# Row maxima by DMA instead of TensorE, and two fp32 products in three rounded passes

## The chip, the cores and the metric

One NeuronCore of a Trainium2 chip runs the whole program; the other cores are idle. The metric is the device time of one execution in microseconds (us), the median over runs. The engines are TensorE (PE in the profile, its weight loads PEld), VectorE (DVE), ScalarE (ACT), GpSimd (POOL) and SyncE (SP), which here only issues DMAs.

## What is computed

The activations are `x`, 4 sequences of 256 tokens with 128 features, and a context of the same shape. Four blocks are added to `x` in turn, each after a layer norm of `x`:

```
x = x + attention0(norm(x), ctx)      # 16 heads of 8 features, softmax over 256 keys
x = x + ffn0(norm(x))                 # 128 -> 512 -> 128; butterflies of 9 stages between, exact gelu
x = x + attention1(norm(x), ctx)      # the same shape as attention0
x = x + moe(norm(x))                  # sigmoid router, best 4 of 16 experts of width 64, and a shared expert
```

The butterfly stages of ffn0 are linear, so the kernel folds them on the chip into one up weight `w_up` and one down weight `w_dn`.

## The kernel before

Everything is kept with features on the partitions and tokens along the free dimension; 1024 tokens are worked in two chunks of 512. Attention is cut into 32 **units** (`unit(U)`): layer, sequence, and a group of four heads that sit in the four 32-row quarters of the PE array. For each unit the program does, in this order:

- `maxima` ("max.U.0", "max.U.1"): four products each, queries on the output partitions, give scores in PSUM whose largest value per query is wanted;
- `reduce` on DVE ("red.U.i"): the negated maximum of each query and head, 128 x 4 values out of 128 x 1024;
- `turn`: eight fp32 products of `T` with the identity, for one or two units at once, turn these maxima from a column per head into rows, so that partition `32j+g` holds the maximum of head j; 17 turns serve the 32 units;
- `shift` on DVE: adds the turned rows to `Q` in place, where `K` has a row of ones, so the next product subtracts the maximum by itself;
- `scores` ("sc.U.0", "sc.U.1"): keys on the output partitions, with the maximum already subtracted;
- `exps` on ACT: four exponentials of 128 x 512 per unit, into `P`, which has room for three units;
- `weighted` ("pv.U"): 8 fp32 products with `V` into the bank `OB`; a copy, a shuffle, a logarithm and an exponential normalise it after each four units.

`Q` and `K` are f32r (rounded fp32), which PE takes in one pass; a plain fp32 product is two passes in the profile. Some products are split to keep precision at f32r speed: the operand is rounded (`k_hi`, `w_hi`), the remainder kept (`k_lo`, `w_lo`), and hi·hi, hi·lo and lo·hi are added in PSUM. `in_parts` does that for the experts' gate and up products. ffn0's up products (`up`), the shared expert's gate-and-up (`gate` with e = 8) and all down products of the experts (`down_product`) are plain fp32 before the change.

In the expert stage there are, for each of two chunks, eight pairs of experts: gate and up products on PE, `silu` on ACT, `prod` on DVE, `hid` (multiplication with the routing weights) on DVE or POOL, and `dn`, which adds into `OB`. `prod_t`, `hid_t` and `gate_t` have two buffers each. The routing weights reach all partitions by a store to DRAM (`comb_out`) and 16 broadcasting loads (`spread`), issued from SP.

The order on each engine is written out by hand in four lists, `PE_ORDER`, `DVE_ORDER`, `ACT_ORDER` and `POOL_ORDER`. A step waits only for the semaphores of what it needs and of the bank that it fills, but an engine never goes past a step that waits. "fill.n" stands for n products of a zero tile that nobody reads, where PE would stand idle. SP issues the first loads, and then nothing until the routing weights.

Of the kernel before, what the change touches and what calls it, by code (L numbers as in the profile page):

```python
# [45 lines left out]
PE_ORDER = """
fill.7:0 centre.0:0 kproj.0.0:1 centre.1:2 avg.0:3 kproj.0.1:4 avg.1:5 fill.1:6 qproj.0.0:6 ksel.0.0.2:0
ksel.0.1.3:3 fill.2:1 qsel.0.0.1:1 ksel.0.0.0:4 ksel.0.1.2:6 qsel.0.0.0:5 ksel.0.1.0:2 ksel.0.0.3:3
ksel.0.0.1:0 ksel.0.1.1:4 max.0.0:56 fill.1:3 max.0.1:23 max.1.0:01 kproj.1.0:4 qsel.0.0.3:5 qsel.0.0.2:6
kproj.0.2:0 max.1.1:56 max.2.0:12 centre.2:3 turn.0:4 qproj.0.1:5 avg.2:6 max.2.1:12 fill.3:3 max.3.0:56  # L50
ksel.1.0.2:3 sc.0.0:01 sc.0.1:24 turn.1:3 max.3.1:56 qsel.0.1.0:2 fill.3:1 max.4.0:34 ksel.1.0.3:1 qsel.0.1.1:2
ksel.0.2.0:0 sc.1.0:56 ksel.1.0.1:1 sc.1.1:34 fill.3:0 max.4.1:23 max.5.0:01 turn.2:6 fw.2:4 vproj.0:23
qsel.0.1.2:5 qsel.0.1.3:6 sc.2.0:01 qproj.0.2:4 fw.1:1 max.5.1:23 ksel.0.2.1:0 ksel.1.0.0:6 sc.2.1:15 pv.0
turn.3:6 sc.3.0:23 qsel.0.2.2:0 max.6.0:45 pv.1 qsel.0.2.0:1 sc.3.1:26 max.6.1:45 sc.4.0:03 pv.2 max.7.0:23
ksel.0.2.2:4 qsel.0.2.1:5 max.7.1:01 fw.0:6 sc.4.1:25 max.8.0:34 pv.3 turn.4:0 sc.5.0:12 max.8.1:56 pv.4
sc.5.1:34 max.9.0:01 ksel.0.2.3:2 kproj.1.1:5 max.9.1:34 sc.6.0:06 qsel.0.2.3:1 pv.5 sc.6.1:02 max.10.0:34
sc.7.0:16 turn.5:5 sc.7.1:02 max.10.1:34 pv.6 ksel.1.1.2:1 max.11.0:56 sc.8.0:02 max.11.1:34 pv.7 max.12.0:56
vproj.1:01 turn.6:3 sc.8.1:45 fw.3:6 sc.9.0:24 max.12.1:01 out.0.0:5 sc.9.1:34 max.13.0:01 pv.8 max.13.1:56
sc.10.0:24 centre.3:3 sc.10.1:01 sc.11.0:24 sc.11.1:56 pv.9 turn.7:0 avg.3:2 max.14.0:45 max.14.1:01 sc.12.0:36
pv.10 pv.11 max.15.0:45 max.15.1:23 up.0.0:6 up.0.3:0 up.0.2:1 up.0.1:2 sc.12.1:36 sc.13.0:45 turn.8:0 down.0:1  # L60
sc.13.1:02 sc.14.0:45 ksel.1.1.1:3 ksel.1.1.0:6 centre.5:1 sc.14.1:04 pv.12 avg.5:6 sc.15.0:25 sc.15.1:04 pv.13
pv.14 qproj.1.0:1 pv.15 ksel.1.1.3:6 qsel.1.0.0:0 fill.4:2 max.16.0:45 max.16.1:12 qsel.1.0.1:0 qsel.1.0.2:6
out.0.1:3 qsel.1.0.3:6 max.17.0:01 max.17.1:45 centre.4:2 max.18.0:01 avg.4:3 turn.9:4 fill.3:5 sc.16.0:56
max.18.1:01 max.19.0:23 up.1.3:4 max.19.1:56 up.1.2:2 up.1.1:3 up.1.0:5 max.20.0:01 sc.16.1:46 max.20.1:23
down.1:5 max.21.0:01 sc.17.0:26 sc.17.1:34 centre.6:5 turn.10:6 max.21.1:01 avg.6:2 max.22.0:45 sc.18.0:36
pv.16 turn.11:0 max.22.1:12 sc.18.1:45 qproj.1.1:3 max.23.0:56 sc.19.0:04 sc.19.1:12 pv.17 qsel.1.1.0:2
max.23.1:34 qsel.1.1.1:0 max.24.0:56 sc.20.0:12 max.24.1:34 pv.18 max.25.0:01 sc.20.1:56 turn.12:2 max.25.1:34
qsel.1.1.2:6 qsel.1.1.3:5 sc.21.0:01 pv.19 sc.21.1:36 max.26.0:01 sc.22.0:24 pv.20 max.26.1:34 sc.22.1:05
sc.23.0:16 pv.21 turn.13:2 max.27.0:34 sc.23.1:05 pv.22 max.27.1:12 sc.24.0:06 pv.23 sc.24.1:35 max.28.0:12
sc.25.0:04 fill.4:6 max.28.1:56 turn.14:3 pv.24 max.29.0:12 max.29.1:56 sc.25.1:04 out.1.0:3 sc.26.0:01  # L70
sc.26.1:24 max.30.0:56 pv.25 turn.15:3 max.30.1:01 sc.27.0:45 centre.7:6 sc.27.1:23 max.31.0:45 avg.7:0
max.31.1:12 sc.28.0:34 sc.28.1:56 pv.26 pv.27 turn.16:0 sc.29.0:12 sc.29.1:36 logits.0:5 gate.0.0:2 sc.30.0:04
sc.30.1:35 pv.28 pv.29 sc.31.0:16 sc.31.1:05 gup.0.0:3 gate.0.1:4 comb.0:0 pv.30 pv.31 gate.0.2:5 gup.0.1:1
gup.0.2:6 gate.0.3:4 gate.0.4:2 gup.0.3:3 gate.0.5:1 out.1.1:0 dn.0.0 dn.0.1 centre.8:4 gup.0.4:5 gate.0.6:6
gup.0.5:2 dn.0.2 avg.8:0 gate.0.7:3 dn.0.3 gate.0.8:1 dn.0.4 gup.0.6:5 logits.1:6 dn.0.5 gup.0.7:2 gate.1.0:4
gate.1.1:0 gate.1.2:5 dn.0.6 gup.1.1:6 comb.1:3 gup.1.0:2 dn.0.7 gate.1.3:4 gate.1.4:2 dn.0.8 gate.1.5:1
gup.1.4:0 gup.1.2:5 gup.1.5:6 gate.1.6:3 gate.1.7:4 dn.1.0 gup.1.3:5 dn.1.1 gup.1.7:2 dn.1.2 dn.1.3 gup.1.6:5
dn.1.4 gate.1.8:1 dn.1.5 dn.1.6 dn.1.7 dn.1.8
"""
DVE_ORDER = """  # L80
xcopy.0 normed.0 klo.0.0 klo.0.1 qlo.0.0 xcopy.1 kev.0.0.2 kev.0.1.2 kev.0.0.3 kev.0.1.0 red.0.0 red.1.0
red.0.1 normed.1 klo.1.0 red.1.1 red.2.0 klo.0.2 qlo.0.1 red.2.1 shift.0 red.3.0 shift.1 red.3.1 red.4.0
kev.1.0.1 normed.2 red.4.1 shift.2 red.5.0 fwr.2 vev.0 qev.0.1.3 qev.0.1.2 fwr.1 red.5.1 qlo.0.2 shift.3
red.6.0 red.6.1 red.7.0 red.7.1 fwr.0 red.8.0 shift.4 red.8.1 red.9.0 shuf.0.0 red.9.1 klo.1.1 red.10.0 shift.5
red.10.1 red.11.0 red.11.1 shuf.0.1 red.12.0 vev.1 shift.6 red.12.1 fwr.3 resid.0.0 red.13.0 red.13.1 shift.7
xcopy.3 red.14.0 normed.3 red.14.1 red.15.1 shuf.0.2 red.15.0 shift.8 ffnadd.0 kev.1.1.0 nmul.0.2 normed.5
qlo.1.0 shuf.0.3 qev.1.0.0 kev.1.1.3 nmul.0.3 red.16.1 red.16.0 resid.0.1 red.17.0 red.17.1 red.18.0 shift.9
normed.4 red.19.0 red.19.1 red.18.1 red.20.0 red.20.1 ffnadd.1 red.21.0 shift.10 red.21.1 red.22.0 normed.6
shift.11 red.22.1 qlo.1.1 red.23.0 red.23.1 red.24.0 red.24.1 red.25.0 red.25.1 shift.12 qev.1.1.3 red.26.0
red.26.1 shuf.1.0 shift.13 red.27.0 red.27.1 ocopy.1.1 shuf.1.1 red.28.0 red.28.1 shift.14 red.29.0 red.29.1  # L90
resid.1.0 red.30.0 shift.15 red.30.1 red.31.0 red.31.1 normed.7 ocopy.1.2 xl.0 shift.16 routing.0 shuf.1.2
wcopy.0 ocopy.1.3 shuf.1.3 prod.0.0 prod.0.1 nmul.1.2 nmul.1.3 prod.0.2 resid.1.1 prod.0.3 hid.0.3 prod.0.4
prod.0.5 xcopy.8 hid.0.5 normed.8 prod.0.6 xl.1 routing.1 prod.0.7 hid.0.7 wcopy.1 prod.1.0 prod.0.8 moeadd.0
prod.1.1 hid.1.0 prod.1.2 prod.1.3 hid.1.3 prod.1.4 prod.1.5 hid.1.4 hid.1.5 prod.1.6 prod.1.7 hid.1.6 hid.1.7
prod.1.8 moeadd.1
"""
# [1135 lines left out]
```

## Time and profile before

| | us |
|---|---|
| median of 3 runs (lowest, highest) | 210.12 (209.35, 210.55) |
| the profiled execution | 209.94 |
| its span in the profile | 207.8 |
| PE busy | 197.7 |
| DVE busy | 154.2 |
| ACT busy | 146.7 |
| POOL busy | 55.6 |

The span lies inside the execution; 2.1 us lie around it. Layer 0's attention and ffn0 run to about 100 us, layer 1's attention from 90 to 160 us, the experts from 160 us to the end. TensorE's granted clock is 1.00 of full speed (2.4 GHz) in all stretches but the last, where the engine has finished.

### The profile page before, as it was taken

The page shows a single profiled execution, that of the slowest core. Times are in us where ns is not written, and L with a number is a line of the kernel's source. Part 1 is how long each engine was busy: PE and PEld are TensorE (multiplying, and loading weights), DVE is VectorE, ACT ScalarE, POOL GpSimd, SP SyncE. Part 2 cuts the span into 40 slices and gives each one's busy share as a digit, 9 for nine tenths or more (in the row PEclk, how much of TensorE's full clock was granted, in tenths as well). Part 3 has the DMA queues.
Part 4 walks back from the last instruction along what each step waited for, and adds up shares of the span by engine and source line. Part 5 has one row for each costly group of instructions (what it writes and reads, how often), then busy time and mean ns, then how long its engine had stood idle before and what let it go on. Part 6 is the DMA issues. An engine that isn't in the chain of part 4 may idle for free.

```text
span 207.8 us, 4287 instructions
## 1 busy us (share of the span) xinstructions
PE 197.7 (95%) x1727; PEld 110.7 (53%) x1727; DVE 154.2 (74%) x243; ACT 146.7 (71%) x262; POOL 55.6 (27%) x72
## 2 busy tenths in 40 slices
PE   7798899999999999997999999999999999999993
PEld 4464367564574543443344566554566745766640
DVE  0399989899998764259975989999775664795482
ACT  2865873989886999972795998987999936613230
POOL 7948940039046000059000000040000252300400
PEclk9999999999999999999999999999999999999999
DMA  6950000000004400000000000000000352003641
GB/s 177 323 224 3 0 0 5 2 3 0 3 0 131 197 3 0 0 5 0 0 0 3 0 5 0 3 0 3 0 5 6 122 205 80 0 6 136 179 142 50
DMA packets 5795, 10.50 MB, mean 51 GB/s; under 512 B 1120, under 2 KB 2576, under 8 KB 5648
## 3 DMA queue, kind: packets, MB, share of 16 engines
q1 hardware_dynamic: 4208, 6.16, 9.3%
q0 software_dynamic: 848, 3.53, 4.5%
q10 hardware_dynamic: 720, 0.53, 0.9%
q8 instruction: 14, 0.23, 0.5%
q14 instruction: 5, 0.04, 0.1%
HBM read 9.64 MB, written 0.59 MB: 49 GB/s over the span
## 4 chain that ended last, share of the span: by engine, by line
PE 81%; DVE 7%; ACT 4%; DMA 2%; issue 2%; SPq 1%; POOL 1%
PE PS L363 60%; PE OB L363 21%; DVE T L1003 3%; DMA spread<-comb_out 2%; SPq L658 1%; DVE attn L1033 1%; DMA comb_out<-comb_t 1%; DVE k_lo L940 1%; DVE xn L991 1%; ACT K L830 1%; POOL hid_t L777 1%; ACT sq L853 1%; ACT sq L856 1%; ACT sq L840 0%; DVE x L1047 0%
## 5 line engine op out<-in xcount | busy, mean ns | idle before, releaser
L1003 DVE TENSOR_REDUCE T<-PS 128x4 f32<-128x1024 f32 x64 | 76.6, 1220 | 4.8 <-PE PS L363 4.2
L864 ACT ACTIVATE P<-PS 128x512 f32<-128x512 f32 x128 | 68.1, 603 | 14.0 <-PE PS L363 13.3
L363 PE MATMUL OB<-P,V 128*32 128x256 f32 x512 | 33.4, 384 | 0.1
L363 PE MATMUL PS<-K,Q 32*128 32x256 f32 x256 | 28.2, 323 | 0.5 <-ACT sq L856 0.3
L363 PEld LDWEIGHTS PS<-K,Q 32*128 32x128 f32 x256 | 17.6, 183 | 17.0 <-ACT P L864 6.9
L363 PE MATMUL PS<-Q,K 32*128 32x256 f32 x256 | 25.6, 320 | 0.3
L363 PEld LDWEIGHTS PS<-Q,K 32*128 32x128 f32 x256 | 16.4, 183 | 11.5 <-ACT P L864 5.1
L777 POOL TENSOR_TENSOR hid_t<-spread,prod_t 128x512 f32<-128x512 f32 x7 | 9.3, 1325 | 46.6 <-DMA spread<-comb_out 37.3
L917 ACT ACTIVATE gate_t<-PS 128x512 f32<-128x512 f32 (+1 forms) x18 | 10.3, 596 | 16.1 <-DVE prod_t L1112 12.0
L363 PEld LDWEIGHTS OB<-P,V 128*32 128x32 f32 x512 | 14.3, 109 | 10.6 <-ACT P L864 0.9
L765 POOL TENSOR_TENSOR attn<-o_raw,sums 128x512 f32<-128x512 f32 x4 | 5.1, 1282 | 44.9 <-ACT sums L883 44.8
L363 PE MATMUL PS<-k_hi,w_hi 128*128 128x512 f32 x32 | 16.7, 522 | 0.0
L363 PE MATMUL OB<-hid_t,w 128*128 128x512 f32 x32 | 16.3, 601 | 0.2 <-POOL hid_t L777 0.2
L1112 DVE TENSOR_TENSOR prod_t<-PS,gate_t 128x512 f32<-128x512 f32 x16 | 10.7, 687 | 7.7 <-PE PS L363 3.9
L1012 DVE TENSOR_TENSOR Q<-PS,Q 128x512 fp32r<-128x512 f32 (+1 forms) x17 | 11.1, 655 | 5.5 <-PE PS L363 5.5
L790 ACT ACT_TABLE_LOAD x10 | 12.8, 1283 | 0.2
L363 PE MATMUL PS<-k_hi,w_lo 128*128 128x512 f32 x32 | 12.6, 393 | 0.0
L363 PE MATMUL PS<-k_lo,w_hi 128*128 128x512 f32 x32 | 12.5, 392 | 0.0
L363 PE MATMUL PS<-cst,T 128*32 128x128 f32 x272 | 10.8, 276 | 0.5 <-ACT K L830 0.3
L991 DVE TENSOR_TENSOR xn<-xn,sq 128x512 f32<-128x512 f32 (+1 forms) x9 | 6.4, 707 | 6.5 <-ACT sq L856 6.4
L840 ACT ACTIVATE sq<-PS 128x512 f32<-128x512 f32 (+1 forms) x9 | 5.0, 550 | 8.8 <-PE PS L363 8.8
L363 PE MATMUL PS<-idle 128*128 128x512 bf16 x31 | 9.9, 439 | 1.2 <-DVE idle L1130 1.2
(125 smaller groups left out, 324.8 us busy)
## 6 DMA issues: line engine op xcount, KB each, us to landing
spread<-comb_out SPq DMA_DIRECT2D x32, 128.0 KB, 3.0
w_gu<-gu POOLq DMA_DIRECT2D x1, 1024.0 KB, 5.5
w<-w2p POOLq DMA_DIRECT2D x1, 512.0 KB, 5.8
outT<-x SPq DMA_DIRECT2D x2, 256.0 KB, 2.9
e_up<-eup POOLq DMA_DIRECT2D x1, 508.0 KB, 6.1
e_dn<-edn POOLq DMA_DIRECT2D x1, 508.0 KB, 6.4
w_exp<-wexp POOLq DMA_DIRECT2D x1, 258.0 KB, 6.2
x<-xT SPq DMA_DIRECT2D x2, 128.0 KB, 3.0
```

The costliest lines, as they stand in the source:

```text
L363: return nc.tensor.matmul(out, lhsT, rhs, start=start, stop=stop)
L658: sp.dma_start(spread[INTER * h:INTER * h + INTER, i % SPREADS, :], comb_out[c, 2 * e + h].partition_broadcast(INTER))\
L765: finish(nc.gpsimd.tensor_tensor(attn[:, :, queries(b)], o_raw[:, k % 2, :].rearrange("p (a q) -> p a q", a=2), sums[:, k % 2, :].rearrang ...
L777: finish(nc.gpsimd.tensor_tensor(hid_t[:, i % 2, :], spread[:, (EPAIRS * c + e) % SPREADS, :], prod_t[:, i % 2, :], ALU.mult), "hid", c, e)
L790: act.preload_act_table_set(name)
L840: nc.scalar.activation(sq[:, lo:hi], bank("centre", n)[:, 0:hi - lo], ACT.Square).then_inc(squared, 1)
L864: finish(nc.scalar.activation(P[:, (JOINT * U + j) % (JOINT * PUNITS), :, :].rearrange("p k q -> p (k q)"), PS[:, FILLED["sc", U, j // 2][ ...
L917: finish(nc.scalar.activation(gate_t[D - rows:D, i % 2, :], bank("gate", c, e)[0:rows, :], ACT.Silu), "silu", c, e)
L991: finish(nc.vector.tensor_tensor(xn[:, lo:hi], xn[:, lo:hi], sq[:, lo:hi], ALU.mult), "normed", n)
L1003: finish(nc.vector.tensor_reduce(dst, two("max", U, i).rearrange("p j (t s) -> p j t s", t=2), AX.X, ALU.max, negate=True), "red", U, i)
L1012: finish(nc.vector.tensor_tensor(dst, bank("turn", t)[:, 0:SEQ].unsqueeze(1).broadcast_to([D, n, SEQ]), dst.bitcast(f32), ALU.add), "shift ...
L1112: finish(nc.vector.tensor_tensor(dst[rows, i % 2, :], src[rows, :], gate_t[rows, i % 2, :], ALU.mult), "prod", c, e)
```

## The change

1. `turn` and `shift` are gone. `T` now keeps the maxima of every unit. Behind the two reduces of a unit, SP stores its 128 x 8 values to DRAM (`turn_out`), waits until they have landed, and loads them into the rows of `Q`. `scores` waits for that load. The DRAM side of the load is read with a step of 32 bytes, so it is made of 1024 separate values of 4 bytes.

```
for U in range(UNITS):
    l, b, g = unit(U)
    for i in (1, 0):
        after(sp, "red", U, i)
    if U >= TURNED:                       # TURNED = 4
        turned_waited(sp, U - TURNED)
    sp.dma_start(turn_out[U], T[:, U, :, :].bitcast(f32)).then_inc(turn_stored, 16)
    sp.wait_ge(turn_stored, 16 * (U + 1))
    sp.dma_start(Q[g:D:32, g, queries(b)].bitcast(f32).rearrange("j (t q) -> j t q", t=2),
                 turn_out[U].rearrange("q j t -> j t q"), allow_slow_non_contiguous=True)\
        .then_inc(turned_in[U % TURNED], 16)
```

```
 def scores(U, i):
-    after(pe, "shift", turned_with(U))
+    turned_waited(pe, U)
```

2. Three passes instead of plain fp32 for ffn0's up (8 products), the experts' down (16) and the shared expert's gate-and-up (2):

```
+def three(to, w_high, w_low, high, low, start=True, stop=True):
+    mm(to, w_high, high, start=start, stop=False)
+    mm(to, w_high, low, start=False, stop=False)
+    return mm(to, w_low, high, start=False, stop=stop)
 def up(c, k):
-    after(pe, "normed", norm(1, c))
+    after(pe, "ulo", c)
-    give(mm(bank("up", c, k), w_up[:, k, :], xn[:, chunk(c)]), "up", c, k)
+    give(three(bank("up", c, k), w_up_hi[:, k, :], w_up_lo[:, k, :], n_hi[:, :], n_lo[:, :]), "up", c, k)
 def down_product(c, e):
-        after(pe, "hid", c, e)
-        w, h = w_2[:, e, :], hid_t[:, i % 2, :]
+        after(pe, "hlo", c, e)
+        last = three(OB[:, :], w_2hi[:, e, :], w_2lo[:, e, :], hid_hi[:, i % 2, :], hid_lo[:, i % 2, :],
+                     start=e == 0, stop=False)
```

The operands are split by new steps: "uhi" (ACT) and "ulo" (DVE) once per chunk for ffn0; "hhi" (12 on ACT, 4 on DVE) and "hlo" (8 on DVE, 8 on POOL) once per pair of experts; "w2split" on POOL splits the weights once, behind "wsplit". `hid_hi` and `hid_lo` have two buffers; "hhi" and "hlo" of a pair wait until the down product two places earlier is done, and "hid" waits for the "hlo" two places earlier.

3. The four order lists are written anew. Beside the removed and added steps, the fills go from 31 to 27 products; DVE takes over 3 copies of `OB`, 4 of the `Q` and 2 of the centring copies from ACT and gives it 1 of the `K` ones; some buffers share their room with others that are dead by then (`n_hi`/`n_lo` lie where `cx` was, `w_2hi`/`w_2lo`/`hid_hi`/`hid_lo` where layer 0's `V` was), which adds waits on long finished steps.

## Rows read from the trace of the kernel before

**Rows 1.** Page, part 1: busy time, share of the span, instructions per engine.
```profile
PE 197.7 (95%) x1727; PEld 110.7 (53%) x1727; DVE 154.2 (74%) x243; ACT 146.7 (71%) x262; POOL 55.6 (27%) x72
```

**Rows 2.** Chain of work that ended last, shares of the span by line.
```profile
by line: PE PS L363 60.0%; PE OB L363 21.3%; DVE T L1003 2.8%; issue 1.9%; DMA spread<-comb_out 1.5%; SPq L658 1.3%; DVE attn L1033 0.9%; DMA comb_out<-comb_t 0.8%; DVE xn L991 0.7%; DVE k_lo L940 0.7%; ACT K L830 0.7%; POOL hid_t L777 0.6%
```

**Rows 3.** Stretches: start:end, length, busy of each engine, clock, DMA share, GB/s.
```profile
30.00:160.00 130.00, 127.44 (x1400) 70.20 (x1392) 104.99 (x154) 107.42 (x195) 23.03 (x24) 1.00 0.04 15
50.00:60.00 10.00, 9.72 (x132) 5.92 (x130) 9.41 (x13) 9.11 (x18) 3.69 (x4) 1.00 0.01 2
70.00:90.00 20.00, 19.89 (x186) 9.02 (x178) 9.44 (x14) 19.14 (x33) 0.00 (x0) 1.00 0.01 3
130.00:140.00 10.00, 10.00 (x164) 5.90 (x156) 9.49 (x14) 9.45 (x19) 2.57 (x2) 1.00 0.01 2
150.00:160.00 10.00, 10.00 (x137) 6.56 (x125) 6.43 (x27) 9.77 (x20) 0.00 (x0) 1.00 0.01 3
```

**Rows 4.** Groups of instructions: count, busy, mean ns, idle time before them.
```profile
L363 PE MATMUL PS<-cst,T 128*32 128x128 f32 x272 | 10.8, 276 | 0.5 <-ACT K L830 0.3 <-DVE k_lo L940 0.2
L1012 DVE TENSOR_TENSOR Q<-PS,Q 128x512 fp32r<-128x512 f32 x15 | 10.3, 687 | 5.1 <-PE PS L363 5.1
```

**Rows 5.** Timeline of PE around one turn: start, length, instructions.
```profile
24.29 0.65 PE L363 MATMUL PS<-cst,T 128*32 128x128 f32 x16 [0.27 <-ACT K L830]
24.87 0.38 PE L363 MATMUL PS<-K,Q 32*128 32x256 f32 x2
25.31 0.82 PE L363 MATMUL PS<-idle 128*128 128x512 bf16 x3
```

**Rows 6.** Chain in order of time, expert stage: start, length, what.
```profile
194.28 0.70 PE PS L363 x3
194.99 0.86 PE OB L363 x2
```

**Rows 7.** The same turning products by stretch: PE busy and count alone.
```profile
50.00:60.00 10.00, 1.29 (x32) 1.00 0.01 2
...
70.00:80.00 10.00, 0.64 (x16) 1.00 0.02 6
...
130.00:140.00 10.00, 1.26 (x32) 1.00 0.01 2
...
150.00:160.00 10.00, 0.62 (x16) 1.00 0.01 3
```

**Rows 8.** Groups of instructions like those added or moved, and the reduces.
```profile
L1065 DVE TENSOR_TENSOR k_lo<-xn,k_hi 128x512 fp32r<-128x512 f32 x2 | 1.4, 682 | 0.0
L901 ACT ACTIVATE k_hi<-xn 128x512 fp32r<-128x512 f32 x2 | 1.3, 631 | 1.6 <-DVE xn L991 1.6
L777 POOL TENSOR_TENSOR hid_t<-spread,prod_t 128x512 f32<-128x512 f32 x7 | 9.3, 1325 | 46.6 <-DMA spread<-comb_out 37.3 <-PE OB L363 4.9 <-DVE prod_t L1112 4.3
```

**Rows 9.** Timeline of DVE and PE at the end of the kernel.
```profile
201.68 0.69 DVE L1122 TENSOR_TENSOR hid_t<-spread,prod_t 128x512 f32<-128x512 f32 x1 [0.71 <-PE OB L363]
200.53 3.03 PE L363 MATMUL OB<-hid_t,w 128*128 128x512 f32 x6
```

**Rows 10.** Timeline of DVE: the first and the last reduces of layer 1.
```profile
94.88 2.34 DVE L1003 TENSOR_REDUCE T<-PS 128x4 f32<-128x1024 f32 x2
148.09 1.23 DVE L1003 TENSOR_REDUCE T<-PS 128x4 f32<-128x1024 f32 x1 [0.43 <-PE PS L363]
```

**Rows 11.** DMA issues: KB each, median us from issue to landing.
```profile
spread<-comb_out SPq DMA_DIRECT2D x32, 128.0 KB, 3.0
comb_out<-comb_t SPq DMA_DIRECT2D x2, 32.0 KB, 1.6
```

**Rows 12.** Timeline of SP's own queue: start, length of the issues.
```profile
160.73 10.99 SPq L658 DMA_DIRECT2D spread<-comb_out  x16
```

**Rows 13.** One 4-byte packet alone in a stretch of 0.05 us: packets, MB, share.
```profile
q1 hardware_dynamic: 1, 0.00, 1.1%
```

**Rows 14.** Stretch 158 to 170 us, the spread loads: packets, MB, share.
```profile
q1 hardware_dynamic: 865, 1.41, 35.1%
```

More of the change, by code:

```diff
@@ L55 @@
[L55 to L69, printed above, removed]
@@ L88 @@
[L88 to L92, printed above, removed]
@@ L118 @@
+hhi.1.5 silu.1.7 hhi.1.6 hhi.1.7 silu.1.8
 """
 POOL_ORDER = """
-expand mixdn mixup nmul.0.0 nmul.0.1 load wsplit nmul.1.0 nmul.1.1 hid.0.0 hid.0.1 hid.0.2 hid.0.4 hid.0.6
-hid.1.1 hid.1.2
+expand mixdn mixup nmul.0.0 load wsplit w2split nmul.1.0 nmul.1.1 nmul.1.2 hid.0.1 hlo.0.0 hid.0.3 hlo.0.2
+hid.0.4 hlo.0.3 hid.0.5 hlo.0.5 hid.0.6 hlo.0.7 hlo.1.0 hlo.1.1 hlo.1.2 hid.1.4 hid.1.6
 """
@@ L462, in maxima @@
                 give(last, "max", U, i)
-            def turn(t):
-                take()
-                for U in reversed(TURN_UNITS[t]):
-                    for i in (1, 0):
-                        after(pe, "red", U, i)
-                if fresh(pe, eye_in, 16):
-                    pe.wait_ge(eye_in, 16)
-                for qt in range(2):
-                    for j in range(JOINT):
-                        rows = slice(32 * j, 32 * j + 32)
-                        last = mm(bank("turn", t)[rows, qt * D:(qt + 1) * D], T[:, t % TURNS, qt, rows], EYE)
-                give(last, "turn", t)
             def scores(U, i):
@@ L901, in high_tokens, with high_rows, high_hidden @@
                 finish(nc.scalar.activation(k_hi[:, chunk(c)], xn[:, chunk(c)], ACT.Copy), "xh", c)
+            def high_rows(c):
+                after(act, "normed", norm(1, c))
+                for v in range(NCH):
+                    filled(act, "vproj", v)
+                for p in range(len(SPANS[1])):
+                    filled(act, "kproj", 1, p)
+                if c:
+                    for k in range(BLK):
+                        filled(act, "up", c - 1, k)
+                finish(nc.scalar.activation(n_hi[:, :], xn[:, chunk(c)], ACT.Copy), "uhi", c)
+            def high_hidden(c, e):
+                i = (EPAIRS + 1) * c + e
+                after(act, "hid", c, e)
+                parts_free(act, c, e)
+                finish(nc.scalar.activation(hid_hi[:, i % 2, :], hid_t[:, i % 2, :], ACT.Copy), "hhi", c, e)
             def router_exp(c):
@@ L1066, in low_tokens, with low_rows, high_hidden, low_hidden @@
                                                ALU.subtract), "xl", c)
+            def low_rows(c):
+                after(dve, "uhi", c)
+                finish(nc.vector.tensor_tensor(n_lo[:, :], xn[:, chunk(c)], n_hi[:, :].bitcast(f32), ALU.subtract),
+                       "ulo", c)
+            def high_hidden(c, e):
+                i = (EPAIRS + 1) * c + e
+                after(dve, "hid", c, e)
+                parts_free(dve, c, e)
+                finish(nc.vector.tensor_copy(hid_hi[:, i % 2, :], hid_t[:, i % 2, :]), "hhi", c, e)
+            def low_hidden(c, e):
+                i = (EPAIRS + 1) * c + e
+                after(dve, "hhi", c, e)
+                parts_free(dve, c, e)
+                finish(nc.vector.tensor_tensor(hid_lo[:, i % 2, :], hid_t[:, i % 2, :],
+                                               hid_hi[:, i % 2, :].bitcast(f32), ALU.subtract), "hlo", c, e)
             def routing(c):
```

268 lines of the change are left out of this document (156 added, 112 removed).

## The prediction

> **What bounds the kernel now.** I read the page's busy times first: PE is busy for 197.7 of 207.8 us, DVE for 154.2, ACT for 146.7 [rows 1]. The reader is to see that nothing but PE can be the bound over the whole. The chain of work agrees: 81% of it is PE's, and no wait for one engine is more than 3% [rows 2]. So what PE no longer does can shorten the kernel nearly in full, if nothing takes its place. The stretches say how far that goes. Between 30 and 160 us PE is busy for 127.4 of 130 us and ACT for 107.4, DVE for 105.0, so on average there is room; but from 50 to 60, 70 to 90, 130 to 140 and 150 to 160 us ACT is busy for 9.11, 19.14, 9.45 and 9.77 us [rows 3]. There PE and ACT are the bound together.
>
> **The turns.** 17 turns of 16 matmul records are removed, 10.8 us of PE [rows 4]. The last records of one overlap what follows: a turn begins at 24.29 and the next product at 24.87 [rows 5], so one is worth 0.58 us, 17 of them 9.9 us. Six stand in the stretches where ACT is full (x32, x16, x32 and x16 records) [rows 7], worth 3.5 us; the idle time of ACT in these 50 us is 50 - 47.5 = 2.5 us [rows 3], so at most 2.5 of the 3.5 can be had. **Gain 8.9 us.**
>
> **The shifts.** 17 additions leave DVE, 15 of them 10.3 us [rows 4]. DVE is no bound on average, so this is booked at nothing; it is the cover for what DVE gets. DVE gets 2 "ulo", 4 "hhi" and 8 "hlo", 14 x 0.68 = 9.5 us by the like operation, and a net 8 copies from ACT (some 5 us); ACT gets 2 "uhi" and 12 "hhi", 14 x 0.63 = 8.8 us, less what it hands over [rows 8]. Both stay near their present sums, 158 and 151 us, but the work moves out of attention into the expert stage, where both have room. If that cover were gone, the price would be these few us once.
>
> **Three passes.** One fp32 product of 512 columns takes 0.86 us of the chain, one split product of three records 0.70 [rows 6]. 8 + 16 + 2 = 26 products at 0.16 are **4.2 us gained**, and all lie on a PE without idle time. **Fills:** three take 0.82 us [rows 5], four fewer give 1.1 us, if the waits that they filled are gone too.
>
> **Longer chains.** Before ffn0's up products stand "uhi" and "ulo", 0.63 + 0.68 us after the norm, twice; scores and maxima of other units stand before them in PE's order, so half is booked, **1.3 us lost**. In the expert stage a pair's chain grows by "hhi" and "hlo", 1.3 us, or 1.9 us where POOL does "hlo" (a POOL operation of that size takes 1.33 us [rows 8]). Behind the waiting "dn" stand the next gates on PE. In the middle gates are placed between. At the end they aren't: now PE and DVE hand over to each other, "hid" of the last pair at 201.68 between down products that begin at 200.53 [rows 9], and moeadd waits for them. So 1.3 us is lost at the end of each chunk, **2.6 us**. "hid" must also wait for the "hlo" two places earlier: hid + hhi + hlo are 2.0 to 3.3 us for two pairs, while PE needs 3 x 0.70 for one pair, 4.2 for two. That is covered. "w2split" on POOL (some 4 operations' work of weights, after wsplit) stands before "nmul" of layer 1 with tens of us to spare: nothing.
>
> **The DMAs.** This is what the trace of before can't show. SP is idle from the first loads until the routing weights, so its queue is free. The nearest rows are the routing weights' own way through DRAM: the store lands in 1.6 us, a load in 3.0 [rows 11]. Behind the second reduce (1.2 us) that is 5.8 us from the last maxima product to the first scores product. In the new PE order a unit's scores stand about three units behind its maxima, and a unit takes now (148.09 + 1.23 - 94.88)/16 = 3.4 us in layer 1 [rows 10], so 9 to 10 us are there; at unit 16, where the order is thinnest, about 6. I book **1.5 us** for the thin places. The size of one 4-byte value isn't in the trace as a load; a 4-byte packet alone took 1.1% of 16 x 0.05 us, or 9 ns [rows 13], and the packets of the spread loads on average 35.1% of 16 x 12 us / 865 = 78 ns [rows 14]. 1024 values over 16 DMA engines are 0.6 us at the one price and 5.0 at the other. I take the lower, since these are 4-byte values too; that is inside the rounding of the 3.0 us, in which the 64 rows of 2 KB of a spread load are contained.
>
> The Trainium skill speaks against this part. "DMA: Bandwidth & Descriptors" (Rules for kernel authors) says that a strided last dimension becomes one descriptor per element, and (Why a DMA increments its semaphore by 16 and not by 1) that a DMA runs on as many of the 16 DMA engines as divide its slowest dimension, which is 4 here. By that the load would be four times longer in its moving part, 2.3 us at 9 ns, an estimate from that page and the row. No run so far shows either.
>
> **Sum.** 8.9 + 4.2 + 1.1 = 14.2 gained; 1.3 + 2.6 + 1.5 = 5.4 lost; and PE idles for 10 us now beside DVE and ACT at three quarters [rows 1], which grows when PE's share falls: I take 1.5 us. 209.94 - 14.2 + 6.9 = 202.6. The profiled execution is 0.2 us under the median, which changes nothing. **Forecast 202.6 us.**
>
> **Rivals.**
> (a) **The gain comes in full.** The waits find cover, the thin places don't wait: 209.94 - 15.2 (9.9 + 4.2 + 1.1) = 194.7, and 197.3 with the 2.6 us at the ends of the chunks, which nothing covers; I take 197. For it: PE is without idle time in most stretches. Against: ACT at 19.14 of 20 us from 70 to 90 and 9.77 of 10 from 150 to 160 [rows 3].
> (b) **Nothing is left.** ACT and the longer expert chains take it all back: 209 to 211. For it: DVE gets 12 more operations in the expert stage, and each down product waits for one more hand-over than before. Against: it needs 5 us more than is booked above, at places that PE doesn't wait at now [rows 2].
> (c) **Slower: the DMA pair becomes the pace of attention.** A unit's store stands behind the load of the unit before it in SP's queue and may not land until that is through. Then a unit takes store and load one after the other, 1.6 + 3.0 = 4.6 us, against 3.4 in layer 1. It decides once a pair takes longer than a unit. 16 x 1.2 = 19 us, less the 3.5 us of lead: 202.6 + 16 = 218 us. If the values cost 4 x 0.6 = 2.3 us instead of 0.6, the pair is 6.3 us, and all 32 units take 202 us, with some 15 us before the first and 45 from 160 us on around them: 262 us. For it: the load is 1024 pieces where the spread load is 64; SP issues 16 of those in 10.99 us [rows 12], 0.69 us each, so many pieces aren't free for SP either. Against: SP itself needs only 1.6 + 0.7 = 2.3 us per unit, and waits for the load of four units earlier only.
> The rule of the page on four engines is the second half of (c), and its chance is in (c)'s.
> (d) That the change doesn't do what it says: a split product could be no faster than a plain one when its operands are fresh. Rows 6 speak against it; 4.2 us less gain, inside the forecast's range.
>
> **How the numbers follow.** Forecast with (d), 199 to 207: 0.40. (a), 194 to 199: 0.15. (b): 0.08. (c) up to 232: 0.22, beyond: 0.15. The most likely is 202.6, with a range of its own of 199 to 207. For 8 in 10 the range leaves out (c) beyond 232 and what lies under 196: 196 to 232. Under 0.5% (1 us), about what a measurement of this kernel can tell from no change: faster 0.57, same 0.07, slower 0.36.
>
> **What would show it.** In the profile after: no matmul PS<-cst,T and no additions to Q; PE's busy sum at 183 to 185 us; down products of 3 records at 0.70 us a product; the load into Q with a median landing near 3 us, and the first records of scores (PS<-K,Q) without waits for it. If (c) is right, PE's share falls to 85% or lower, PE waits for "DMA Q<-turn_out" in each unit of layer 1, and reduces come at the pace of the DMA pair. If ACT is what takes the gain, it is busy for over 9.5 of 10 us in most stretches from 30 to 150 us. The prediction is wrong in its main step if a load takes more than about 4 us to land, or if stores land much later than 1.6 us because loads are before them.

## The result: slower by 17%

The changed kernel takes **249.08 us** (median of 4 runs, 246.04 to 252.13) against 210.34 for the kernel before beside it, a ratio of **1.1725 [1.1642, 1.1809]**. The forecast was 202.6 us, the range 196 to 232: the sign was wrong and the time lies outside. The medians are of all runs, the ratios here and below only of a kernel's fast ones, which is why 249.08/210.34 isn't 1.1725. The profiled execution took 246.44 us, span 244.6.

The page, busy times and granted clock in 40 slices; these answer to [rows 1]:

```profile
PE 209.9 (86%) x1477; PEld 119.1 (49%) x1477; DVE 163.6 (67%) x249; ACT 149.0 (61%) x266; POOL 70.7 (29%) x83
...
PEclk9999999756967999999999755877866799999999
```

PE issues 250 records fewer and is busy longer, for a smaller share of the span. In some slices the mean granted clock lies below the full 2.4 GHz, down to half of it, the lower of its two levels.

The kernel in stretches, cut at the same marks in each kernel: the start of the first exponential, of the last one of layer 0, of the first of layer 1, of unit 24's first, of the last one, and the store of the routing weights. Columns: start:end, length, busy of PE, PE's weight loads, DVE, ACT, POOL, then the clock, the DMA share and GB/s. First before:

```profile
24.10:88.50 64.40, 63.67 (x711) 35.99 (x712) 50.07 (x75) 54.62 (x101) 16.51 (x18) 1.00 0.08 28
88.50:102.90 14.40, 12.63 (x91) 5.69 (x89) 12.15 (x14) 7.75 (x15) 7.84 (x8) 1.00 0.01 2
102.90:135.30 32.40, 32.08 (x358) 17.24 (x354) 27.66 (x30) 28.15 (x49) 0.00 (x0) 1.00 0.01 2
135.30:157.40 22.10, 21.97 (x270) 13.02 (x267) 19.32 (x42) 19.75 (x41) 2.57 (x2) 1.00 0.01 2
...
159.10:207.80 48.70, 45.27 (x168) 26.78 (x160) 29.15 (x60) 20.70 (x32) 9.27 (x7) 0.99 0.31 99
```

Then after:

```profile
20.70:97.80 77.10, 69.04 (x587) 39.62 (x587) 52.06 (x74) 53.76 (x98) 18.78 (x20) 0.87 0.19 25
97.80:113.90 16.10, 13.57 (x79) 5.28 (x71) 12.67 (x15) 6.34 (x11) 11.85 (x12) 1.00 0.05 2
113.90:154.50 40.60, 36.69 (x294) 19.18 (x298) 27.61 (x30) 27.28 (x48) 1.27 (x1) 0.79 0.14 3
154.50:188.40 33.90, 24.40 (x208) 12.66 (x208) 19.05 (x40) 20.33 (x40) 1.27 (x1) 0.75 0.13 3
188.40:195.20 6.80, 6.80 (x63) 3.88 (x63) 1.98 (x4) 2.24 (x5) 1.27 (x1) 0.72 0.00 0
195.20:244.60 49.40, 41.95 (x171) 29.35 (x169) 37.79 (x68) 24.60 (x40) 20.66 (x15) 0.99 0.32 98
```

The attention of layer 0 grew from 64.4 to 77.1 us, that of layer 1 from 54.5 to 74.5. The first exponential came 3.4 us sooner. The expert stage, where the three passes should pay, grew by 0.7 us. SP's queue (start, length of the issue): the first pair of the kernel, three loads of layer 1 with their stores, and the last load:

```profile
14.53 0.33 SPq L665 DMA_DIRECT2D turn_out<-T  x1
15.94 0.68 SPq L667 DMA_DIRECT2D Q<-turn_out  x1
...
137.37 0.53 SPq L667 DMA_DIRECT2D Q<-turn_out  x1
138.01 1.82 SPq L665 DMA_DIRECT2D turn_out<-T  x1
142.32 0.54 SPq L667 DMA_DIRECT2D Q<-turn_out  x1
143.35 1.48 SPq L665 DMA_DIRECT2D turn_out<-T  x1
147.29 0.54 SPq L667 DMA_DIRECT2D Q<-turn_out  x1
...
181.46 0.54 SPq L667 DMA_DIRECT2D Q<-turn_out  x1
```

A load goes out as soon as its store has landed. The first store took 1.41 us; behind a load it takes 142.32 - 138.01 = 4.31. From load to load the median of 31 distances is 4.95 us.

The profile gives no landing for these loads, but where TensorE waits for one, its next scores product starts when the load has landed:

```profile
147.23 0.79 PE L363 MATMUL PS<-Q,K 32*128 32x256 f32 x4 [1.16 <-DMA Q<-turn_out]
...
186.08 0.92 PE L363 MATMUL PS<-Q,K 32*128 32x256 f32 x8 [1.93 <-DMA Q<-turn_out]
```

The load issued at 142.32 has landed by 147.23, 4.91 us later, and the store behind it is through at 147.29, with it. Of the 13 such waits twelve give 4.2 to 4.9 us for a load, one 6.7. The last load, issued at 181.46, has no store behind it and still takes 4.62. So the load alone is the long part, and the store behind it lands when the load does. Who waits, over the whole span (us in total, times, longest):

```profile
PEld PS L363 <- issue: 46.5, 78, 4.8
ACT P L906 <- PE PS L363: 36.9, 31, 5.4
...
DVE T L1057 <- PE PS L363: 27.9, 25, 4.9
PE PS L363 <- DMA Q<-turn_out: 18.9, 13, 4.0
```

PE waits for loads, and ACT and DVE wait for PE. That is rival (c), though not to the letter of its signs: PE's share is 86% and not 85% or lower, and PE itself waits in 13 places and not in each unit. The experiments ask whether it is the whole cause, and where the gains went. Kernel before in their comparisons: 211.0 to 211.5 us.

### The profile page after: what moved, and what is told of

The parts are those of the page before. It is cut to its first block and busy times, and to the rows that moved or that the text cites. A ratio compares the mean times of both kernels' runs of the same rounds, so it can differ in the third digit from the quotient of the medians.

```text
span 244.6 us, 3948 instructions
## 1 busy us (share of the span) xinstructions
PE 209.9 (86%) x1477; PEld 119.1 (49%) x1477; DVE 163.6 (67%) x249; ACT 149.0 (61%) x266; POOL 70.7 (29%) x83
## 2 busy tenths in 40 slices
DMA packets 43299, 10.75 MB, mean 44 GB/s; under 512 B 38624, under 2 KB 40080, under 8 KB 43152
## 5 line engine op out<-in xcount | busy, mean ns | idle before, releaser
L1057 DVE TENSOR_REDUCE T<-PS 128x4 fp32r<-128x1024 f32 x64 | 76.7, 1221 | 28.4 <-PE PS L363 27.9
L363 PE MATMUL PS<-Q,K 32*128 32x256 f32 x256 | 31.2, 370 | 20.0 <-DMA Q<-turn_out 18.9
L363 PE MATMUL OB<-P,V 128*32 128x256 f32 x512 | 42.3, 467 | 0.0
L363 PEld LDWEIGHTS PS<-Q,K 32*128 32x128 f32 x256 | 20.5, 222 | 34.5 <-issue 19.7
L363 PE MATMUL PS<-K,Q 32*128 32x256 f32 x256 | 34.9, 357 | 1.0 <-DVE Q L1018 0.4
L363 PEld LDWEIGHTS PS<-K,Q 32*128 32x128 f32 x256 | 23.0, 213 | 23.4 <-issue 8.8
L803 POOL TENSOR_TENSOR hid_lo<-hid_t,hid_hi 128x512 fp32r<-128x512 f32 x8 | 10.9, 1371 | 10.0 <-ACT hid_hi L961 7.2
L961 ACT ACTIVATE hid_hi<-hid_t 128x512 fp32r<-128x512 f32 x12 | 7.4, 632 | 9.4 <-POOL hid_t L819 4.2
L363 PE MATMUL PS<-k_hi,w_lo 128*128 128x512 f32 x32 | 12.7, 398 | 0.0
L363 PE MATMUL PS<-k_lo,w_hi 128*128 128x512 f32 x32 | 12.7, 398 | 0.0
L363 PE MATMUL PS<-sq,cst 128*128 128x512 f32 (+1 forms) x18 | 9.5, 612 | 2.5 <-ACT sq L882 1.5
L363 PE MATMUL PS<-attn,w_o 128*128 128x512 f32 x16 | 9.6, 733 | 1.5 <-DVE attn L1078 1.5
```

Of the source, the lines that this page charges most:

```text
L363: return nc.tensor.matmul(out, lhsT, rhs, start=start, stop=stop)
L803: finish(nc.gpsimd.tensor_tensor(hid_lo[:, i % 2, :], hid_t[:, i % 2, :], hid_hi[:, i % 2, :].bitcast(f32), ALU.subtract), "hlo", c, e)
L961: finish(nc.scalar.activation(hid_hi[:, i % 2, :], hid_t[:, i % 2, :], ACT.Copy), "hhi", c, e)
L1057: finish(nc.vector.tensor_reduce(T[:, U, 2 * i:2 * i + 2, :], two("max", U, i).rearrange("p j (t s) -> p j t s", t=2), AX.X, ALU.max, nega ...
```

## The experiments on the DMAs

**Loads into a spare tile.** The scores wait for none.

```
- sp.dma_start(Q[g:D:32, g, queries(b)]...
+ sp.dma_start(spare[g:D:32, :]...
- turned_waited(pe, U)          # scores
```

> The changed kernel, but the loads of the maxima land in a spare tile and no scores product waits for them (the output lacks the subtraction of the maxima). All DMAs stay. Theory A (the DMA pair is the pace, through the wait of scores alone): PE no longer waits, its clock stays at 1.00, the span falls from 244.6 to 195-205 us while SP still needs about 5 us per unit. Theory B (the traffic itself slows the other engines, or the new order and the longer chains cost the time): it stays above 225 us.

226.16 us, ratio 1.0703 [1.0614, 1.0791]: theory B's number. The trace says that its reason is a third one. SP's queue at the end of attention:

```profile
170.30 0.53 SPq L667 DMA_DIRECT2D spare<-turn_out  x1
170.88 1.98 SPq L672 DMA_DIRECT2D comb_out<-comb_t  x1
```

and the stretch that follows, columns as above:

```profile
170.00:180.00 10.00, 0.00 (x0) 0.00 (x0) 1.12 (x2) 0.00 (x0) 0.00 (x0) 0.50 0.29 73
```

The last exponential started at 155.3 us. The 32 pairs, at nearly 5 us each, keep SP until 170.8, and the store of the routing weights stands behind them. For ten us PE does nothing. Until then the attentions had taken 63.5 and 54.6 us, as in the kernel before (64.4 and 54.5).

**The same without the last five pairs.**

```
- for U in range(UNITS):
+ for U in range(UNITS - 5):    # SP only
```

> The kernel with loads into a spare tile (scores wait for none, rows of Q keep no maxima, output not the reference's), and besides SP skips the two DMAs of the last five units; everything else, so 27 of the 32 pairs with their 4-byte pieces, is as in that run, which took 226.2 us. Theory A, SP's queue is late: in that run's trace the last load is issued at 170.30 us and the routing weights' store behind it at 170.88, against 157.36 where there are no such DMAs, and TensorE idles from about 168 to 183 us. With five pairs of 4.95 us fewer SP is free about when the weights are ready: the store goes out at 157 to 160 us and the total is 208 to 213. Theory B, the 4-byte traffic slows the engines: 27 of 32 pairs stay, so 223 to 226.

209.75 us (one run). SP's queue:

```profile
143.61 0.54 SPq L667 DMA_DIRECT2D spare<-turn_out  x1
158.53 0.34 SPq L672 DMA_DIRECT2D comb_out<-comb_t  x1
```

27 pairs with all their small pieces cost next to nothing where no product waits for them; 16 us were the late queue. No slowing of the engines by the traffic is seen.

**No DMAs of maxima at all.**

```
- sp.dma_start(turn_out[U], T[:, U, :, :]...)   # SP's whole loop over units
- sp.dma_start(Q[g:D:32, g, queries(b)]..., turn_out[U]...)
- turned_waited(pe, U)
```

> As the one before, and the 64 DMAs of the maxima are not issued at all (the output lacks the subtraction of the maxima). Theory A: within 1 us of the one before, 195-205 us. If the 4-byte traffic costs something beside the wait: faster than the one before by more than 2 us.

210.25 us, ratio 0.9875 [0.9789, 0.9961]. It misses 195 to 205, and that it is 16 us faster than with the loads into a spare tile is the late queue again, not a cost of the traffic. So the turning through DRAM costs about 39 us (249.1 against 210.3, ratios 1.1725 against 0.9875), and all the rest of the change brings 1% where I had booked 14.2 us of gains and 3.9 of chains.

**Whole rows.** Only the load's shape changes: 4 pieces of 1 KB.

```
- Q[...].rearrange("j (t q) -> j t q", t=2), turn_out[U].rearrange("q j t -> j t q")
+ Q[...], turn_out[U].rearrange("q j t -> (q j t)").rearrange("(j n) -> j n", j=JOINT)
```

> The changed kernel with the load in 4 pieces of 1 KB instead of 1024 of 4 bytes (the rows get the maxima in a wrong order); every wait stays. Theory A1 (the pieces are the pace, about 1.5 us in motion and as much again until they count as landed): the pair falls to about 1.4 + 2.2 = 3.6 us or less, PE's waits nearly vanish, 198-208 us. Theory A2 (a pair through DRAM is too slow whatever its pieces: store 1.6 + load 3.0 us): the pace stays at 4 us or more, 215-230 us.

208.67 us, ratio 0.9856 [0.9757, 0.9955], just above the range of A1. Way through DRAM, waits and queue are all still there; the 1024 pieces are gone and with them 40 us. SP's queue:

```profile
129.94 0.32 SPq L665 DMA_DIRECT2D turn_out<-T  x1
131.35 0.50 SPq L667 DMA_DIRECT2D Q<-turn_out  x1
132.24 0.32 SPq L665 DMA_DIRECT2D turn_out<-T  x1
133.65 0.50 SPq L667 DMA_DIRECT2D Q<-turn_out  x1
```

The store lands in 1.41 us again and the pair can follow every 2.3 us, faster than the units come.

**512 pieces of 8 bytes.**

```
- Q[...].rearrange("j (t q) -> j t q", t=2), turn_out[U].rearrange("q j t -> j t q")
+ Q[...].rearrange("j (q t) -> j q t", t=2), turn_out[U].rearrange("q j t -> j q t")
```

> The changed kernel with the load in 512 pieces of 8 bytes in the place of 1024 of 4 bytes, same bytes, same rows, same waits (the two values of one query side by side, so the order in the row is wrong and the output is not the reference's). Theory A, the pace goes by the number of pieces: 1024 pieces give 4.95 us from load to load and 4 pieces 2.1 us at the least, that is 2.8 ns a piece, so 512 give about 3.5 us; since the scores of layer 1 need a pair in each 3.4 us, the total is 212 to 225. Theory B, a fixed cost of an out-of-order load (any piece under some size, or the source's scattered addresses): 244 to 252 as with the change itself.

211.8 us (one run): the same bytes in half the pieces, and nearly the whole loss is gone. Median landing of a store 1.7 us against 4.1; where pairs follow closely they do so in 3.05 us. In four places where TensorE waits for such a load, it has landed 3.1 to 3.3 us after its issue. That is theory A's mechanism, at a time just under its range. The cost in the end time isn't proportional to the pieces: where the pair is shorter than a unit's 3.4 us [rows 10] it costs next to nothing, above that every unit pays.

**Stores by POOL.** Units 20 to 31 only.

```
+ nc.gpsimd.dma_start(turn_out[U], T[:, U, :, :]...).then_inc(pool_stored[U - 20], 16)
  # SP: waits for pool_stored[U - 20], issues the load
```

> The changed kernel, whole computation, with the stores of units 20 to 31 issued by POOL on its own queue in the place of SP's; SP only waits for them and issues the loads. Theory A, rival (c) of the prediction: a store stands in its queue behind the load before it, and the pair is the pace (4.95 us; packets of a load are in motion for 1.5 us only). With the stores elsewhere the loads' pace from unit 20 on falls to 3.4 us or less, what ScalarE needs for a unit, and the total to 226 to 238. Theory B, a load of 1024 pieces occupies the queue or the issue for nearly all of the 4.95 us by itself: pace over 4.4 us, total 243 to 252. POOL's own store costs more to issue and land than SP's (not measured so far), which can add to the time of the last unit.

236.77 us (one run), clock 0.935, in theory A's range. The twelve loads from unit 20 on go out from 132.21 to 171.24 us, 3.5 us apart in the mean in the place of 4.95; some follow each other by under 2 us, which a store between them in the queue did not allow. Layer 1 from its first exponential on, same marks as above:

```profile
117.50:154.00 36.50, 31.90 (x295) 17.08 (x300) 27.43 (x29) 26.97 (x48) 5.04 (x8) 0.96 0.17 3
154.00:179.90 25.90, 22.25 (x207) 11.52 (x207) 18.94 (x40) 20.06 (x39) 3.94 (x6) 0.83 0.17 3
```

From unit 24 on 25.9 us instead of 33.9, before 22.1. With the same loads of 1024 pieces, the store's place behind them was two thirds of the loss there (8.0 of 11.8 us; the clock is higher too, 0.83 against 0.75). The rest goes with PE's waits for loads, still 5.8 us from 130 us on: a load on a queue without stores still takes up to 4.6 us to land. (Up to unit 19 nothing is changed, and POOL's store itself takes 2.5 us to land.)

**What a piece costs.** DMA engines between the load issued at 137.37 us and the next (40 slices of 0.125 us: busy share in tenths of 16 engines):

```profile
DMA  0000000000013333333333343000000000000000
...
q1 hardware_dynamic: 1172, 0.01, 13.0%
```

13.0% of 16 x 5.0 us over 1172 packets is 8.9 ns a packet: [rows 13] had the piece right. The load's pieces start 1.4 us after its issue, move for about 1.5 us, and the 128 pieces of the store, and 20 more, come at their end, until 140.5. The store counts as landed at 142.32, 1.8 us later. So the pair is 1.4 (issue of the load to its first piece) + 1.5 (its pieces) + 0.2 (the store's) + 1.8 (landing). The 1.8 us are not what a store needs by itself: the first store of the kernel moves its last packet at 15.55 us and counts as landed at 15.94, 0.4 us later. They belong to the load, which lands at the same moment; why its landing comes so long after its last piece, no run shows. "DMA: Bandwidth & Descriptors" in the Trainium skill (Anatomy of one DMA, on DMAs that GpSimd issues) puts most of a DMA's fixed cost of about 2 us in the confirmation of the last write; here 1.8 us lie behind the last packet in one case and 0.4 us in the other, so the trace agrees with it for the load and not for the store alone. The rule of the same page of the Trainium skill that a strided last dimension becomes one descriptor per element (Rules for kernel authors) agrees with the packets of the whole kernel, 43299 against 5795. The four engines aren't decided: 1024 pieces at 8.9 ns in 1.5 us are 6 engines' worth, if no two of an engine overlap.

**The small pieces on the store's side.** Load of 4 whole rows, the whole computation.

```
- sp.dma_start(turn_out[U], T[:, U, :, :]...)
+ sp.dma_start(turn_out[U].rearrange("j t q -> q j t"), T[:, U, :, :]...)
```

> The changed kernel with the turning moved from the load to the store: the store writes 1024 values of 4 bytes from 128 partitions, the load reads 4 whole rows of 1 KB. Full result. Theory A1 with the pieces bound to the 4 partitions of the load: the store's pieces go out over all DMA engines in 0.4 us, pair about 4 us or less, 198-210 us. If 4-byte writes are slow wherever they go: the store lands after 4-5 us and the time stays near 245 us.

417.91 us, ratio 1.973 [1.9561, 1.99]. Far beyond both expectations. A store's landing, min/median/max:

```profile
DMA to landing us min/median/max: 8.1/9.7/12.4
```

The pair takes 10.4 us (median from load to load) against 4.95 with the small pieces in the load. "VectorE: DVE Perf Modes" in the Trainium skill (The three transpose paths) warns that a plain DMA that transposes by its strides is 19 times slower than the transposing hardware where the destination's inner stride is large. No run here uses that hardware or shows that ratio, but the side that the page names, the destination, is the dear one here: 9.7 us for such a store, 4.2 to 4.9 for the load with the stride on its source.

**Turning by VectorE, in blocks of 32 by 32.** Whole computation; the load takes whole rows.

```
+ nc.vector.transpose(TT[:, U % 4, :], T[:, U % 4, :])    # 128 x 32
+ sp.dma_start(turn_out[U].rearrange("c b q -> b c q"), TT[:, U % 4, :])
```

> The changed kernel with the whole computation, but the turning done in another way: VectorE transposes the maxima of a unit in blocks of 32 by 32 (one instruction of 32 columns for each unit), the store writes rows of 32 values, and the load fetches four whole rows. No 4-byte pieces are left, both DMAs and all waits stay. Theory A, the 1024 pieces of 4 bytes are the pace: the load's pair falls from 4.95 us to about 2.1 to 2.5 us as with whole rows, and the total is that run's 208.7 plus what 32 short VectorE instructions cost (VectorE is busy 79% there; 32 at 0.1 to 0.2 us are 3 to 6 us, a part of them beside other waits): 208.5 to 213. Theory B, what costs is to get the values in turned order through DRAM at all, or the waits of the scores: 225 to 250.

215.5 us, ratio 1.0241 [1.0093, 1.0388], 2.5 us over the expectation. One group of VectorE:

```profile
L1060 DVE STREAM_TRANSPOSE TT<-T 128x32 f32<-128x32 f32 x32 | 6.8, 212 | 3.2 <-DVE T L1050 0.5
```

6.8 us of work and 3.2 of idle time ahead of it are 10 us on DVE; the kernel is 6.8 us slower than with whole rows. Pieces of 128 bytes free the queue (a pair takes 2.5 us at the least), and what is lost fits DVE's 10 us in size; that these are the cause was not tested by itself.

**Pieces of 8 bytes in the right order.** Whole computation.

```
- Q[rows, g, q0:q0 + D]                        # columns of the maxima's products
+ Q[rows, g, b * SEQ + qt:b * SEQ + SEQ:2]
```

> The changed kernel with pieces of 8 bytes and the whole computation: the products of the maxima take every second column of Q (queries 2q and 2q+1 of a unit beside each other in T), so that the load's 512 pieces of two values land in the right order. Everything else as in the change. From the run with 512 pieces in the wrong order (211.8 us): 210 to 214. The other way: weight loads with a step of two columns are slower, which is on TensorE's path 256 times; then 215 or more.

211.91 us, ratio 1.0043 [0.999, 1.0096], as expected. This repairs the change: computing what it computes, it is as fast as the kernel before. It doesn't beat it.

**Fills against the clock.** Three idle products ahead of each unit's first scores.

```
- sc.U.0:ab
+ fill.3:a sc.U.0:ab      # U = 0 to 31
```

> The changed kernel with three more filling matmuls ahead of each unit's first scores (idle data, 32 times three), so that TensorE has work while it waits for a load. Theory A, the low granted clock in stretches 50:60 (0.55) and 140:150 (0.50) is a consequence of TensorE's waits and costs nothing of its own, since the pace of the loads sets the end: 246 to 253 with a granted clock over 0.95. Theory B, the clock is a second cause (TensorE is busy 209.9 us against 187.3 us for the same products in the whole-rows run): then fills win a part of it back, 236 to 243. The fills themselves are 96 products, up to 0.2 us each where they do not lie in waits.

251.96 us (246.71 to 253.45) at a clock of 0.95 to 0.975 instead of 0.88 to 0.90: theory A. A higher clock in the attention brings nothing back, since the loads set the pace; what the fills cost themselves was not measured apart. At one place the low clock does cost. Between the last exponential and the store of the routing weights PE is busy throughout, with 63 records: 6.8 us at 0.72 in the changed kernel, 7.0 at 0.70 here, 5.7 at 0.86 in the run with POOL's stores.

## The experiments on the gains

**Plain fp32 products again**, on top of whole rows.

```
- three(bank("up", c, k), w_up_hi, w_up_lo, n_hi, n_lo)
+ mm(bank("up", c, k), w_up, xn[:, chunk(c)])        # so too gate.8 and down_product
- uhi ulo hhi hlo w2split
```

> The kernel of the run with whole rows (load in 4 pieces of 1 KB, values in the wrong order, so the output is not the reference's), and besides the three-pass products of the change taken back: up, the gate of the shared expert and the experts' down products are plain fp32 matmuls again, without the splits into high and low parts. The whole rows alone gave 208.67 us. Theory A, my prediction's term: 26 products save 0.16 us each on TensorE, 4.2 us, minus about 2 us for chains, so this kernel is slower, 210.5 to 213. Theory B: in the expert stage TensorE is no longer the bound with three passes, since in the whole-rows trace its idle time from 156 to 206 us is 8.2 us against 3.4 us from 159 to 208 us of the kernel before, and the conversions of each expert's rows stand on the chain: then taking them back changes little or helps, 206.5 to 209.5, with TensorE busy over 45 us in the expert stage and DVE and POOL less.

207.88 us, ratio 0.9865 [0.9816, 0.9913], against 208.67 and 0.9856 for whole rows with three passes: no difference in the whole time that is clear of the noise. Nine of the ten runs lie between 205.87 and 210.59 us; the tenth took 435.21, which nothing here explains. One thing more was changed than the expectation says: `hid_t` has four buffers here and two there. The expert stage with three passes:

```profile
156.00:205.50 49.50, 41.81 (x171) 29.39 (x169) 37.79 (x68) 24.57 (x40) 20.93 (x15) 0.99 0.31 98
```

and with plain products:

```profile
158.90:206.60 47.70, 44.02 (x153) 26.49 (x151) 28.93 (x56) 17.58 (x28) 9.30 (x7) 1.00 0.31 101
```

Three passes take 2.2 us off PE, and the stage is 1.8 us longer: PE idles 7.7 us there instead of 3.7. They cost DVE 8.9, ACT 7.0 and POOL 11.6 us. Part of the 1.8 can be the two buffers less, but the sign holds without them: with plain products and two buffers, in the old order, the stage takes 48.2 to 48.7 us in four traces, with three passes 49.2 us or more in each trace of this document.

**The kernel before without its turns and shifts.**

```
- turn.0 ... turn.16 (PE)   - shift.0 ... shift.16 (DVE)
- after(pe, "shift", turned_with(U))
```

> The kernel before with its 17 turns and 17 shifts left out and nothing else changed: rows of Q keep no maxima, so the output is not the reference's; scores wait for nothing in their place. Theory A, the term of my sum: each turn is worth 0.58 us on TensorE, 8.9 us in all, so about 202 (200 to 203.5). Theory B: most of that time lies beside ScalarE's or VectorE's full stretches and passes on to waits for them: in the whole-rows run the last exponential ends 5.5 us earlier than in the kernel before, with TensorE idle 3.0 us in layer 1 against 0.5, so here 204.5 to 208.

213.3 us, ratio 1.0119 [1.0077, 1.0161]: **slower** than with them, against both theories. Stretches, the same marks:

```profile
25.40:89.40 64.00, 60.92 (x583) 33.61 (x584) 45.58 (x67) 54.20 (x101) 15.14 (x17) 1.00 0.08 28
...
103.00:139.30 36.30, 34.98 (x294) 17.52 (x294) 26.23 (x26) 28.27 (x50) 0.00 (x0) 0.86 0.01 1
139.30:161.20 21.90, 21.12 (x221) 11.99 (x219) 17.55 (x39) 19.61 (x40) 2.55 (x2) 1.00 0.01 1
```

At the full clock nothing is won: layer 0 takes 64.0 us instead of 64.4, the end of layer 1 21.9 instead of 22.1, with PE busy 2.8 and 0.9 us less. The stretch between them runs at 0.86 and takes 36.3 instead of 32.4. (Another at 0.66, from 10 to 20 us, lies ahead of the first turn and can't come from their absence.) What the removed work leaves are waits. DVE's reduces and PE's weight loads, before and without turns:

```profile
PEld PS L363 <- DVE T L1003: 7.3, 14, 0.9
...
DVE T L1003 <- PE PS L363: 4.2, 10, 0.8
```

```profile
DVE T L996 <- PE PS L359: 16.7, 25, 2.0
...
PEld PS L359 <- DVE T L996: 11.1, 17, 1.5
```

**One idle product for each turn.**

```
- turn.0:4 ... turn.16:0
+ fill.1:4 ... fill.1:0     # shifts left out as above
```

> The kernel before without turns and shifts, and in the place of each turn one idle filling product (bf16, 512 columns, about 0.2 us at the full clock, 17 in all); rows of Q keep no maxima, so the output is not the reference's. Without the fills it took 213.3 us, with a granted clock of 0.66 to 0.76 in three stretches. Theory A, the clock took a gain back: with fills the clock stays at 0.99 or more and the time falls to 204 to 208. Theory B, the turns lay beside other waits and no gain was there to take back: 209.5 to 213, whatever the clock.

212.11 us, ratio 0.998 [0.9932, 1.0029]; theory B, and the four runs at 0.991 and more took 209.4 to 210.8 us, not 204 to 208. Its clock was 0.94 to 0.998 from run to run, so runs can be compared at one clock. For the kernel before, 51 runs beside these experiments lie on a line with a scatter of 0.5 us: 0.01 of mean clock goes with 1.4 us, and at 0.99 it takes 210.8. The lines of the others give there: without turns 209.6 (its runs reach 0.972 only, so this is extended), with one fill each 210.5, whole rows 209.0, whole rows with plain fp32 207.9, pieces of 8 bytes 211.9. At 0.957, where there are runs of both, the kernel without turns takes 213.1 to 213.7 us and the kernel before 215.4 to 215.5. So 17 turns and shifts are worth some 1 to 2 us at an equal clock, and the clock takes more than that: without turns its mean is 0.957 in the middle of ten runs, against 0.989 for the kernel before, some 4 us. One idle product for each turn raises it to 0.976. What sets off a stretch at a low clock in one run and not in another stays open.

**Twice the products in each turn.**

```
+ for _ in range(8):
+     last = mm(bank("turn", t)[0:32, 256:256 + D], T[:, t % TURNS, 0, 0:32], EYE)
```

> The kernel before with twice the products in each turn (8 more calls, 16 more instructions for each of 17 turns, into an unused part of the same bank; the output is the reference's). By the price of the prediction, 0.58 us for a turn on a TensorE that is the bound, 8.9 us more: 219 to 221. By theory B, a turn's work lies beside waits: 211 to 215.

237.69 us, ratio 1.127 [1.118, 1.136]: 26.5 us more, beyond both theories. The added products all use one group of rows of the array and run one after the other, so they are dearer than the expectation took them for. The turning products of the whole kernel, where [rows 4] had 272 in 10.8 us:

```profile
L363 PE MATMUL PS<-cst,T 128*32 128x128 f32 x544 | 40.1, 274 | 0.1
```

That is 29.3 us more of PE, 1.7 us for each turn in the place of 0.58, and the kernel grew by 26.5. Work added at a turn's place is paid at nine tenths; work taken away there brings 1 to 2 of 9.9 us. I read this as a balance: the order, laid out with the turns in it, has PE, DVE and ACT meet at their banks. What in the order makes it one was not tested.

## The prediction, point by point

- **What bounds the kernel.** PE's 95% and its 81% of the chain were read rightly, and work added to it costs nine tenths of its time. "No wait for one engine is more than 3%" was not: [rows 2] go by line, and by engine DVE has 7% of that chain and ACT 4%. The inference failed: "what PE no longer does can shorten the kernel nearly in full". The 10 us of idle time in [rows 1] were all the slack that the waits behind PE showed, and a chain that passes from PE to PE doesn't say how close the others are. DVE (9.49) and ACT (9.45) of 10 us in [rows 3] did.
- **The turns, -8.9 us.** The term that was most off on this side: about -1 to -2 at an equal clock, and +2 with the clock's loss in the kernel before. I limited it only in stretches where ACT is over 9 of 10 us, 2.5 us of idle time there; the gain stayed small everywhere.
- **The shifts, nothing.** DVE's busy sum came to 163.6 us and ACT's to 149.0, against the 158 and 151 named. The 1.3 us before ffn0's up products and the 1.1 us of fills were not tested apart.
- **The clock** stood in no term. The stretches of [rows 3] show 1.00 with PE busy in every stretch. With PE's work taken out, its waits grew, and stretches at 0.73 and 0.76 followed. PE's busy sum, said to be 183 to 185 us, was 209.9 in the changed kernel and 187.3 with whole rows, where the clock was 0.997.
- **Three passes, -4.2 us; their chains +2.6.** The size per product was near (busy -2.2 us for 18 products in the expert stage, 0.12 each against 0.16), the chains too small: the stage became 0.7 to 1.8 us longer (49.4 in the changed kernel and 49.5 with whole rows, against 48.7 before and 47.7 with plain products and four buffers) where the sum had it shorter. In the whole time the sum of both terms is not clear of zero. "hid" and "hlo" take 1.4 us each on POOL, 1.33 in [rows 8], and PE waits in between, not only at the ends of chunks. Rival (d) is false, and in the expert stage (b) happened.
- **The order.** What all of the change but its DMAs brings, 1.2 to 1.4%, can't be laid to the turns alone, since without them the old order got slower: the first exponential comes 3.5 us sooner with the changed order (20.6 us with whole rows) but not without turns in the old order (25.4). What in the order does it wasn't isolated.
- **The DMAs, +1.5 us.** This decided the result: +39. Four estimates stood in it. The piece, 9 ns: right, 8.9 measured. Its spread over engines: 1.5 us in motion, between the 0.6 taken and the 2.3 worked out from the rule in the Trainium skill ("DMA: Bandwidth & Descriptors", Why a DMA increments its semaphore by 16 and not by 1). The load's landing, 3.0 us, taken from a spread load and said to contain the pieces: wrong, 4.2 to 4.9 us, with or without a store behind it. By the prediction's own sign, over 4 us, its main step fails there. (The scores products that wait are PS<-Q,K in the trace, not PS<-K,Q.) The store, 1.6 us: wrong, 4.1 in the median, since it lands only with the load ahead of it. I had this mechanism in (c), with the right place, queue and point of decision (3.4 us a unit), priced the pair at 4.6 or 6.3, and measured is 4.95. That 4.6 is near is partly luck: it adds a store of 1.6 to a load of 3.0, where the load takes nearly all of it and the store lands beside it. The time of (c), 218, was too low since I took 16 units of layer 1 alone to pay, 1.2 us each; layer 0 lost 12.7 us as well, and the store of the routing weights came only 6.8 us after the last exponential, at a clock of 0.72.
- **Choosing against (c)** was the step at fault. The argument for it, pieces that aren't free, had a row; the argument against, that SP needs only 2.3 us for two issues, assumed that the store's 1.6 us hold behind a load, which no row showed. The measured pair, 4.95 us, is over the 3.4 us of a unit, so the 1.5 us booked for thin places became 39. The chance of 0.37 with a range that ended at 232 left its worse half out.
